# Relative-position attention and a ternary MLP on one core: score blocks of two neighbouring heads in one half step, and jobs placed ahead of the value products

## The reference, cut to what matters

```python
xn = layernorm(x)                              # plain
a  = layernorm(xn) * ln_g + ln_b               # inside the attention
q, k, v = a@Wq+bq, a@Wk+bk, a@Wv+bv            # 16 heads of 8 columns
p  = sinusoidal_pe(512, 128) @ Wp              # the same for all batches
content = einsum(q + u_bias, k)                # 512 x 512 per head
pos     = relative_shift(einsum(q + v_bias, p))
attn    = softmax((content + pos) * 8**-0.5)
att_out = (attn @ v) @ Wo + bo
h = relu(s0 * [xn, -xn] @ (+-1 matrix)) * 2    # 512 wide
h = relu(s1 * h @ (+-1 matrix)) * 2            # 512 wide
out = x + att_out + s2 * h @ (+-1 matrix)
```

## Time and profile before

| | |
|---|---|
| median of three runs | 1802.21 us |
| profiled execution | 1803.9 us |
| its span in the trace | 1802.1 us |
| TensorE matmuls busy | 1721.8 us, 96% |
| VectorE busy | 1429.6 us, 79% |
| ScalarE busy | 1256.5 us, 70% |
| GpSimd busy | 750.4 us, 42% |
| moved by DMA | 563.49 MB, mean 313 GB/s |

### The profile page before, as it was taken

How to read it: one execution, slowest core, us unless ns; L and a number is a source line. 1 busy time by engine, 2 the same in 40 slices (tenths; PEclk the granted TensorE clock), 3 DMA queues, 4 the chain that set the end, 5 groups by cost and what they waited for, 6 DMA issues and landing times.

```text
span 1802.1 us, 40835 instructions
## 1 busy us (share of the span) xinstructions
PE 1721.8 (96%) x15720; PEld 1015.2 (56%) x15720; DVE 1429.6 (79%) x3545; ACT 1256.5 (70%) x1333; POOL 750.4 (42%) x743
## 2 busy tenths in 40 slices
PE   5999999999999999999999999999999999999894
PEld 2466555655655555555555555555555555555563
DVE  2378888888888888887888888888877888888684
ACT  2577777777777777777677777777677777777652
POOL 5753634445353443535344362444434344333100
PEclk9999999999999999999999999999899999999987
DMA  2989999999999999999899999999999999999980
GB/s 96 309 286 325 344 322 332 329 334 330 328 338 314 328 325 329 336 323 337 304 332 335 330 339 321 331 322 342 298 332 322 321 332 341 330 330 317 349 288 25
DMA packets 96626, 563.49 MB, mean 313 GB/s; under 512 B 12208, under 2 KB 22192, under 8 KB 30896
## 3 DMA queue, kind: packets, MB, share of 16 engines
q10 hardware_dynamic: 36864, 268.45, 45.9%
q1 hardware_dynamic: 59568, 292.43, 44.9%
HBM read 282.96 MB, written 277.87 MB: 311 GB/s over the span
## 4 chain that ended last, share of the span: by engine, by line
PE 75%; DVE 11%; POOL 5%; DMA 4%; SPq 2%; issue 2%; ACT 1%; POOLq 0%; ACTq 0%; DVEq 0%
PE ps_pt L590 23%; PE ps_pos L571 14%; PE ps_av L604 12%; PE ps_job L545 12%; PE ps_job L509 7%; DVE sc_sb L475 4%; DVE sums_t L494 3%; POOL x_sb L222 3%; PE ps_job L512 2%; DMA sums_t<-heads_d 2%; DVE sc_sb L480 2%; PE ps_con L581 2%; SPq L264 1%; DMA heads_d<-o_sb 1%; PE ps_job L520 1%
## 5 line engine op out<-in xcount | busy, mean ns | idle before, releaser
L475 DVE CUSTOM_DVE_ANT_0 sc_sb<-ps_con,sc_sb 128x512 f32<-128x512 f32 x1024 | 659.9, 681 | 269.8 <-PE ps_con L581 267.0
L381 ACT COPY pos_sb<-ps_pos 128x1024 f32<-128x1024 f32 x512 | 519.8, 1015 | 207.0 <-PE ps_pos L571 202.1
L480 DVE TENSOR_SCALAR sc_sb<-sc_sb,nmax 128x512 f32<-128x512 f32 x1024 | 644.5, 670 | 0.0
L590 PE MATMUL ps_pt<-c_sb,sc_sb 128*128 128x128 f32 x4096 | 569.8, 283 | 2.1 <-ACT pt_sb L389 2.1
L389 ACT ACTIVATE pt_sb<-ps_pt 128x1024 f32<-128x1024 f32 x512 | 524.8, 1025 | 66.4 <-PE ps_pt L590 60.1
L590 PEld LDWEIGHTS ps_pt<-c_sb,sc_sb 128*128 128x128 f32 x4096 | 448.2, 143 | 184.6 <-issue 143.5
L581 PE MATMUL ps_con<-k_stack,q_stack 26*128 26x512 f32 x1024 | 395.8, 457 | 24.5 <-DVE nmax L475 20.6
L571 PE MATMUL ps_pos<-p_stack,q_stack 26*128 26x512 f32 x1024 | 390.0, 458 | 3.2 <-ACT pos_sb L381 2.7
L604 PE MATMUL ps_av<-pt_sb,v_sb 128*9 128x128 f32 x8192 | 326.8, 278 | 8.2 <-DVE o_sb L486 7.7
L571 PEld LDWEIGHTS ps_pos<-p_stack,q_stack 26*128 26x128 f32 x1024 | 158.4, 189 | 288.2 <-issue 271.5
L321 POOL CAST h<-act_sb 128x512 fp32r<-128x512 f32 x128 | 83.2, 650 | 464.6 <-ACT act_sb L362 464.1
(11 more groups left out here) (63 smaller groups left out, 934.2 us busy)
## 6 DMA issues: line engine op xcount, KB each, us to landing
shift<-pos_sb SPq DMA_DIRECT2D x256, 1026.0 KB, 7.9
sc_sb<-shift ACTq DMA_DIRECT2D x256, 1024.0 KB, 8.5
heads_d<-o_sb SPq DMA_DIRECT2D x64, 72.0 KB
x_sb<-in_x SPq DMA_DIRECT2D x16, 256.0 KB, 6.6
o_t<-heads_d SPq DMA_DIRECT2D x16, 256.0 KB, 7.4
sums_t<-heads_d SPq DMA_DIRECT2D x128, 32.0 KB, 5.9
out<-x_sb SPq DMA_DIRECT2D x16, 256.0 KB, 8.3
stack_w_sb<-in_stack_w SPq DMA_DIRECT2D x1, 512.0 KB, 5.3
```

The costliest lines, as they stand in the source:

```text
L381: act.copy(pos_sb[:, u % N_POS, 2 * i:2 * i + 2, 1:PITCH], ps_pos[:, :, :]).then_inc(s_pe, 1)
L475: dve.tensor_tensor_reduce(sc_sb[:, m % N_SC, t, :], ps_con[:, t % 2, :], sc_sb[:, m % N_SC, t, :], -SCALE, 3.4e38, ALU.add, ALU.min, nmax ...
L480: dve.tensor_scalar(sc_sb[:, m % N_SC, t, :], sc_sb[:, m % N_SC, t, :], nmax[:, m % N_SC, t:t + 1], None, ALU.subtract).then_inc(s_sub, 1)
L590: last = pe.transpose(ps_pt[:, j % 2, t * P:(t + 1) * P], sc_sb[:, u % N_SC, t, j * P:(j + 1) * P], id_sb)
```

## The change

1. **Blocks.** In a half step the two position blocks belong to two neighbouring units and so do the two content blocks (`blocks`): block `i+2` of unit u-1 and block `i` of unit u. A unit is spread over four half steps, 2u to 2u+3, one block in each. The four matmuls of a half step are on the four different row groups. The wait of `positions` for `s_pe` stands once ahead of all four.
2. **Lags.** The write of a unit waits two half steps longer, the load back is issued at 2u+8 instead of 2u+6, the first content block stays at 2u+12, the transposes go from 2u+15 to 2u+17, and heads, reciprocals, `WO` and `TY` move by two half steps.
3. **Buffers.** `pos_sb` has four units instead of three; `x1_t` has one batch instead of two.
4. **ScalarE's copy** takes one block of each of two units; it is one instruction as before, with a computed step between them.
5. **VectorE** does the same four instructions per half step, on blocks of two units; the last transposes' wait counts one instruction fewer.
6. **Jobs** run between `turn` and `values` instead of after `values`.
7. **Tables.** The jobs of a batch have other half steps. The half steps without a job are 10, 11, 16, 19 and 26 before, and 7, 22, 26, 27 and 28 after.

```diff
@@ -28,13 +28,14 @@
     PITCH = S + 1
 
 
-    SHIFT_LAG = 3
+
+    SHIFT_H = 8
     CONTENT_LAG = 6
-    TURN_H = 2 * CONTENT_LAG + 3
+    TURN_H = 2 * CONTENT_LAG + 5
     VALUES_H = TURN_H + 1
-    HEADS_SLOT = CONTENT_LAG + 2
+    HEADS_SLOT = CONTENT_LAG + 3
     N_X = 4
-    N_POS = 3
+    N_POS = 4
     N_SC = 6
     N_SHIFT = 6
     N_PT = 4
@@ -90,7 +91,7 @@
         mv = sb("mv", [P, 2, NT, 2])
         var_eps = sb("var_eps", [P, 2, NT])
         rstd = sb("rstd", [P, 2, NT])
-        x1_t = sb("x1_t", [P, 2, 2, S], F32R)
+        x1_t = sb("x1_t", [P, 2, S], F32R)
         z_t = sb("z_t", [P, S])
 
         QS = sb("q_stack", [P, GROUPS, S], F32R)
@@ -171,14 +172,14 @@
         FIRST = ((0, "T1", 0), (0, "V", 0), (1, "QG", 1), (2, "PG", 1), (3, "KG", 1), (4, "QG", 2), (5, "PG", 2),
                  (6, "L0", 0), (7, "KG", 2), (8, "L0", 1), (9, "L0", 2), (10, "L0", 3), (11, "PG", 3),
                  (12, "QG", 3), (13, "L1", 0), (14, "L1", 1), (15, "KG", 3), (18, "L1", 2), (19, "L1", 3),
-                 (29, "L2", 0, 2))
-        FIRST_NEXT = ((16, "T1", 0), (17, "TZ", 0), (20, "QG", 0), (21, "L0", 0), (22, "V", 0), (23, "KG", 0),
-                      (24, "L0", 1), (25, "L0", 2), (26, "L0", 3), (28, "QG", 1))
-        LAST = ((27, "WO", 0), (28, "TY", 0))
-        THIS = ((0, "L1", 0, 2), (3, "KG", 1), (4, "QG", 2), (5, "L1", 1, 2), (7, "KG", 2), (8, "L1", 2, 2),
-                (12, "QG", 3), (13, "L1", 3, 2), (15, "KG", 3), (30, "L2", 0, 2))
-        NEXT = ((2, "T1", 0), (17, "TZ", 0), (18, "L0", 0), (20, "QG", 0), (21, "L0", 1), (22, "V", 0),
-                (23, "KG", 0), (24, "L0", 2), (25, "L0", 3), (29, "QG", 1))
+                 (31, "L2", 0, 2))
+        FIRST_NEXT = ((16, "T1", 0), (17, "TZ", 0), (20, "L0", 0), (21, "L0", 1), (22, "L0", 2), (23, "QG", 0),
+                      (24, "V", 0), (25, "KG", 0), (26, "L0", 3))
+        LAST = ((29, "WO", 0), (30, "TY", 0))
+        THIS = ((1, "QG", 1), (2, "L1", 0, 2), (4, "KG", 1), (5, "L1", 1, 2), (8, "QG", 2), (9, "L1", 2, 2),
+                (12, "L1", 3, 2), (14, "KG", 2), (15, "QG", 3), (16, "KG", 3), (31, "L2", 0, 2))
+        NEXT = ((11, "T1", 0), (17, "TZ", 0), (18, "L0", 0), (19, "L0", 1), (20, "L0", 2), (21, "L0", 3),
+                (23, "QG", 0), (24, "V", 0), (25, "KG", 0))
         for half, name, c in START:
             add(half - 32, name, 0, c)
         for it in range(B + 1):
@@ -215,6 +216,24 @@
         def half_of(h, lag):
             k = h - lag
             return divmod(k, 2) if 0 <= k < 2 * UNITS else (None, None)
+
+        def blocks(h, lag):
+
+            u, i = divmod(h - lag, 2)
+            return [(v, t) for v, t in ((u - 1, i + 2), (u, i)) if 0 <= v < UNITS]
+
+        def content_end(u):
+            return 2 * u + 3 + 2 * CONTENT_LAG
+
+        def score_halves(h):
+
+            return min(max(h + 1, 0), 2 * UNITS + 2)
+
+        def scored(h, lag):
+
+            k = h - lag
+            return 0 if k < 0 else min(k + 1, 2) + 2 * max(min(k, 2 * UNITS - 1) - 1, 0) \
+                + min(max(k - 2 * UNITS + 1, 0), 2)
 
         def scale_rows(eng, b, k):
             src, dst = ((x_sb[:, b % N_X], x1_sb), (x1_sb, z_sb))[k]
@@ -263,9 +282,9 @@
                     for d in range(DH):
                         sp.dma_start(sums_t[H * d:H * d + H, :],
                                      heads_d[P:P + H].rearrange("p t c -> p (t c)")).then_inc(s_hr, 16)
-                u = unit(n, 0)
+                u = unit(n, 1)
                 if u is not None:
-                    sp.wait_ge(s_pe, 2 * (u + 1))
+                    sp.wait_ge(s_pe, score_halves(2 * u + 3))
                     if u >= N_SHIFT:
                         v = u - N_SHIFT
                         sp.wait_ge(s_in[v % N_SC], 16 * (v // N_SC + 1))
@@ -308,13 +327,13 @@
                                        "PG": (PS, LOW_K, s_ps)}[name]
                     dst = dst[:, c, :]
                     if b > 0:
-                        pool.wait_ge(s_con, NT * (H * (b - 1) + GROUP * (c + 1)))
+                        pool.wait_ge(s_con, scored(content_end(H * (b - 1) + GROUP * (c + 1) - 1), 2 * CONTENT_LAG))
                     own(pool.tensor_tensor(dst, src, low.broadcast_to([P, S]), ALU.mult))
                     pool.tensor_tensor(dst, src, dst.bitcast(F32), ALU.subtract).then_inc(s_hl, 1)
                     pool.wait_ge(s_hl, k + 1)
                     pool.sem_inc(ready, 1)
                 else:
-                    dst, read = {"T1": (x1_t[:, b % 2], job("L0", b - 2, C1 - 1)),
+                    dst, read = {"T1": (x1_t[:, :, :], job("L0", b - 1, C1 - 1)),
                                  "L0": (h1[:, c], job("L1", b - 1, C2 - 1)),
                                  "L1": (h2[:, c], job("L2", b - 1))}[name]
                     wait(pool, s_job, read)
@@ -366,19 +385,26 @@
                 last.then_inc(s_jev, 1)
 
             for h in HALVES:
-                u, i = half_of(h, 2 * SHIFT_LAG)
+                u, i = half_of(h, SHIFT_H)
                 if i == 0:
                     act.wait_ge(s_out_w[u % N_POS], 16 * (u // N_POS + 1))
                     wait(act, s_pt, 2 * (u - N_SC + 1))
                     act.dma_start(sc_sb[:, u % N_SC].rearrange("p t c -> p (t c)"),
                                   shift[u % N_SHIFT, S:S + S * S].rearrange("(p c) -> p c", p=P)) \
                        .then_inc(s_in[u % N_SC], 16)
-                u, i = half_of(h, 0)
-                if u is not None:
-                    act.wait_ge(s_pos, h + 1)
-                    if i == 0 and u >= N_POS:
-                        act.wait_ge(s_out_w[u % N_POS], 16 * (u // N_POS))
-                    act.copy(pos_sb[:, u % N_POS, 2 * i:2 * i + 2, 1:PITCH], ps_pos[:, :, :]).then_inc(s_pe, 1)
+                todo = sorted(blocks(h, 0), key=lambda v: v[0] % N_POS)
+                if todo:
+                    act.wait_ge(s_pos, score_halves(h))
+                    for u, t in todo:
+                        if t == 0 and u >= N_POS:
+                            act.wait_ge(s_out_w[u % N_POS], 16 * (u // N_POS))
+                    to = [pos_sb[:, u % N_POS, t, 1:PITCH] for u, t in todo]
+                    if len(to) == 2:
+                        to = bass.AP(tensor=to[0].tensor, offset=to[0].offset,
+                                     ap=[to[0].ap[0], [to[1].offset - to[0].offset, 2], [1, S]])
+                        act.copy(to, ps_pos[:, :, :]).then_inc(s_pe, 1)
+                    else:
+                        act.copy(to[0], ps_pos[:, 0, :]).then_inc(s_pe, 1)
                 u, i = half_of(h, TURN_H)
                 if u is not None:
                     k = 2 * u + i
@@ -466,19 +492,19 @@
             for h in HALVES:
                 n = h // 2
                 it, slot = n // 16, n % 16
-                m, i = half_of(h, 2 * CONTENT_LAG)
-                if m is not None:
-                    if i == 0:
+                todo = blocks(h, 2 * CONTENT_LAG)
+                before = scored(h - 1, 2 * CONTENT_LAG)
+                for k, (m, t) in enumerate(todo):
+                    if t == 0:
                         dve.wait_ge(s_in[m % N_SC], 16 * (m // N_SC + 1))
-                    for t in (2 * i, 2 * i + 1):
-                        dve.wait_ge(s_con, NT * m + t + 1)
-                        dve.tensor_tensor_reduce(sc_sb[:, m % N_SC, t, :], ps_con[:, t % 2, :],
-                                                 sc_sb[:, m % N_SC, t, :], -SCALE, 3.4e38, ALU.add, ALU.min,
-                                                 nmax[:, m % N_SC, t:t + 1]).then_inc(s_ttr, 1)
-                    for t in (2 * i, 2 * i + 1):
-                        dve.wait_ge(s_ttr, NT * m + t + 1)
-                        dve.tensor_scalar(sc_sb[:, m % N_SC, t, :], sc_sb[:, m % N_SC, t, :],
-                                          nmax[:, m % N_SC, t:t + 1], None, ALU.subtract).then_inc(s_sub, 1)
+                    dve.wait_ge(s_con, before + k + 1)
+                    dve.tensor_tensor_reduce(sc_sb[:, m % N_SC, t, :], ps_con[:, k, :],
+                                             sc_sb[:, m % N_SC, t, :], -SCALE, 3.4e38, ALU.add, ALU.min,
+                                             nmax[:, m % N_SC, t:t + 1]).then_inc(s_ttr, 1)
+                for k, (m, t) in enumerate(todo):
+                    dve.wait_ge(s_ttr, before + k + 1)
+                    dve.tensor_scalar(sc_sb[:, m % N_SC, t, :], sc_sb[:, m % N_SC, t, :],
+                                      nmax[:, m % N_SC, t:t + 1], None, ALU.subtract).then_inc(s_sub, 1)
                 o, i = half_of(h, VALUES_H)
                 if i == 1 and o % 4 == 3:
                     dve.wait_ge(s_av, 2 * (o + 1))
@@ -532,7 +558,7 @@
                         return pe.transpose(dst, src[:, t, :], id_sb)
                     return [lambda t=t: block(t) for t in range(NT)]
 
-                w, src, before = {"L0": (w0, x1_t[:, b % 2].unsqueeze(1), [("T1", b, 0)]),
```

(38 more changed lines are left out.)

## The result

The changed kernel takes 1744.9 us in the median (1742.4 to 1746.1), the kernel before beside it 1803.1 us: a ratio of 0.967, with a 95% interval of 0.964 to 0.970. It is 58 us faster. The forecast was 1758, in a range of 1712 to 1803: right in direction, and 13 us short of the gain. The profiled execution spans 1743.7 us.

A forecast was written before the change was run, and what follows sets the result against it. TensorE was taken to bound half steps with MLP jobs; batch work summed to 100.5 us, under a 102.1 transfer floor, plus 2.2 irregular: 104.3. 1802.1 - 14 x 2.7 - 5 - 3 + 2 gave 1758 us, range 1712 to 1803.

The forecast's parts named there:

- Score blocks: TensorE's four score matmuls per half step: 0.40 us instead of 0.66, gaining 0.26 us, 8.3 us a batch.
- Rival 3: Score matmuls: four row groups do not run together, scores stay at 0.66 us; about 1803 us, chance 0.10.
- Jobs ahead of the values cost TensorE nothing (the same instructions): TensorE's job order: moving jobs between transposes and value products was put at no cost.
- `L0` half steps at 2.7: Half steps 18 to 21: ScalarE needs 2.72 us against TensorE's 2.55, so 0.7 us a batch are not gained.
- The reciprocals: VectorE around half steps 24 to 28: extra work there loses 1.5 us a batch, bounds 0 and 3.9.
- I raise the irregular part from 1.7 to 2.2: Irregular waits per batch, coming with transfers: 2.2 us instead of 1.7, added to the regular 102.1 to give 104.3.
- The floor of 102.1 us: DMA engines: with share stuck at 0.97 and packet durations kept, a batch can't be under 0.97 x 105.3 = 102.1 us.
- The test that the forecast named for being wrong: DMA engines: forecast wrong if the share stays at 0.97 while the batch shortens, or landing goes up to 12 us.
- Rival 1: Transfers: they are elastic and waits rare, so a batch is 102.2 us; 1729 us, chance 0.18.
- Rival 2: ScalarE and VectorE: reading PSUM out becomes the bound, a batch is 106.6 us; 1790 us, chance 0.13.
- Rival 4: VectorE's wait for `sc_sb` at a unit's first block: loads come too late, batch 108.8 us; 1821 us, chance 0.12.
- Ends: Outside the regular batches: first batch 5 us off, last batch 3 off, tail 2 us on.

The follow-up runs named there:

- the later place: Changed kernel with reciprocals, their product, WO, TY and L2 two half steps later, and jobs from QG 1 to L0 3 mostly one later: 1712.9 us, 0.950.
- the best version: Changed kernel with sums and what follows two half steps later, and the L0 jobs after the value products: 1706.9 us, 0.943.

## Why the forecast came out

It came out in part by luck: terms that it missed on both sides nearly cancel. Its total per batch (104.3) is the measured one (104.4), but not by its own working.

- **Score blocks: right.** 0.44 us, near the 0.40 taken, 0.22 a half step instead of 0.26. Rival 3 is out: without the row groups the kernel is 84 us slower. The Trainium skill's 3.07 gave 0.37 as an estimate ("TensorE: Matmul & The Clock Gate", Part 3); measured is a little more, up to the first full-array instruction.
- **"Jobs ahead of the values cost TensorE nothing (the same instructions)": wrong**, the step that failed most plainly. It counted instructions and not what stands beside them (why the neighbours matter is only in part shown, see above). It is a gain of 0.15 to 0.2 us in each half step with a job other than `L0`, -26 us on the kernel before and -40 us on the changed one.
- **Half steps without a job at 2.27: right** away from the stall, 2.21 at half step 7 and 2.30 at 22. The other three, 26 to 28, stand behind the stall of half step 25 and take 3.6, 2.7 and 2.7. The forecast had said over 2.6 there, but for the reciprocals' own work.
- **`L0` half steps at 2.7: wrong in the engine.** They were costed on ScalarE, and take 3.3 to 3.5 on VectorE beside GpSimd. The forecast had the price of the subtractions beside a split, but counted it once in a sum of loads that it held equal to before; where in the half step the split falls decided. Cost: 2.6 us a batch (13.5 us for the four, 10.9 forecast).
- **The reciprocals (1.5, at most 3.9 us) and "I raise the irregular part from 1.7 to 2.2": the largest term mis-sized.** The reciprocal itself is cheap; waiting for the sums ahead of it costs VectorE 5.8 us in the median batch (102.9 us in 16 places). The step that failed treated the present 28.3 us as transfers being now and then late. In truth the path from `o_sb` to the reciprocal had no slack (23.3 us under a cover of 22.6), and the change keeps its distance in half steps while it lengthens the path to 27.4 and shortens the cover to 21.6.
- **The norm: wrong, at no cost.** "The norm should be done in time": VectorE waits 40.0 us in 15 places, 41.3 before.
- **The floor of 102.1 us: too high by some 2%, and not what held this kernel.** The test that the forecast named for being wrong is met: over batches 2 to 13 the share is 0.96 in both kernels, while the batch goes from 107.0 to 104.4 us. So the packets did not keep their durations: 0.96 x 104.4 = 100 us of them a batch, under the 102.1 taken. The changed kernel's 104.4 is held by the sums: it falls to 102.2 without their loads, 101.7 with the later place. But there a bound of the forecast's kind appears, just under its number: at 101.7 the share is 0.99, in the best version 1.00 at 100.0 (98.7 at best), and with a quarter of the bytes gone the batch is 97.3. Rival 1 (1729 us) was nearer on the transfers and was kept from coming true by the sums.
- **Rival 2** gets its share in the `L0` half steps. **Rival 4** is out: VectorE waits for `sc_sb<-shift` once, for 0.3 us, as the landing is 9.5 us and not 13. With the later sums it begins to show, at a landing of 11.3: 6.9 us in 12 places.
- **Ends: too careful.** The forecast had 6 us off for both together; 14.9 + 8.8 - 5.0 = 18.7 are measured. The 13 us beyond the forecast lie here: batches 1 to 14 gave 39.8 against 37.8. In half steps 17 to 31 of batch 0 the order and the scores work 15 times before any sums are waited for (54.8 us to 46.7).

Still open: why the new tables and lags by themselves raise the sums' last landing from 5.9 to 9.7 us, in a kernel that moves the same bytes in more time. That the landing depends on the traffic beside it is shown by the run with half writes, and 396 GB/s go beside it in the changed kernel. One guess is that the new lags put a 1 MB write or load just there. The traces do not bear it out as it stands. In the kernel before, the load back is issued 0.4 us ahead of the first read of the heads in the median, with tables and lags only 0.8 us behind it, in the changed kernel 1.7 ahead. And in three batches of the kernel before it is issued 0.2 to 0.5 us behind as well, and the sums have all landed 10.4 to 11.9 us after the first read, no later than in its other batches. No run moved one of these transfers alone.

## What to carry to other kernels

Count on TensorE not only instructions, but also what stands next to what (row groups, full array, column groups); an order that puts pieces of one kind together is worth a trial. When a loop is made shorter, list every path whose distance is counted in iterations, and convert it to microseconds of the new iteration: a round trip over HBM doesn't shrink with it, and may grow. A total that comes out right proves none of its terms; look at each.

## What the runs showed of the hardware

- A half step in which the full-array job stood beside the full-array transposes, and not between the column-group values and the row-group scores, was 0.15 to 0.2 us shorter: 3.37 to 3.17 us, 3.14 to 2.94 us, and 2.99 with the job at the other side of the transposes.
- Four 26-row matmuls on four row groups start within 0.01 us and hold TensorE for 0.44 us, against 0.66 for two groups twice.
- VectorE's fp32 subtraction from SBUF to SBUF took 2.27 us for two beside a GpSimd split, instead of 0.87; its read of a PSUM bank stayed at 0.68 beside one.
- Mixed writes and reads of 1 MB went at 354 GB/s at a share of 1.00 over 493 us, and at 396 over a stretch of 10.5.
- After 5.1 us without matmuls the granted clock read 0.52 for the next 6 us, and transposes took 1.97 us instead of 1.09.
